# Wide cross attention on one core: the output projection of two batches at once, transposed, and turned back

## The reference, cut to what matters

```python
def _L1_xattn_ref(x, context, ln_gamma, ln_beta, Wq, Wkv, Wo, bo, mask):
    ...
    xn = (x - mu) * jax.lax.rsqrt(var + LN_EPS) * ln_gamma + ln_beta
    q = xn @ Wq                      # 256 -> 1024
    kv = context @ Wkv               # context: 361 rows of 192
    ...
    dots = jnp.einsum('bhnd,bhmd->bhnm', q, k) * scale
    dots = jnp.where(mask, dots, -jnp.inf)
    attn = jax.nn.softmax(dots, axis=-1)
    out = jnp.einsum('bhnm,bhmd->bhnd', attn, v)
    out = out.transpose(0, 2, 1, 3).reshape(x.shape[0], x.shape[1], INNER)
    return out @ Wo + bo             # 1024 -> 256
...
x = x + _L1_xattn_ref(_layernorm(x, axis=-1), ctx_768, ...)
```

## Time and profile before

| | us |
|---|---|
| three runs | 3828.05, 3830.51, 3836.60 (median 3830.51) |
| the profiled execution | 3829.01 |
| its span of engine work | 3827.2 |
| PE busy in the span | 3591.3 (94%) |
| PE's granted clock, mean of the span | 0.965 of full speed |
| DVE, ACT, POOL busy | 1925.8, 1614.7, 1558.3 |

### The profile page before, as it was taken

The page is one execution under the profiler, slowest core; times in us unless marked ns, Lnnn a source line. Parts: engine busy times, 40 slices in busy tenths (PEclk is TensorE's granted clock), DMA queues, the critical chain, the costliest instruction groups (busy, mean ns, idle before and its releaser), DMA issues. The chain is left out here.

```text
span 3827.2 us, 70846 instructions
## 1 busy us (share of the span) xinstructions
PE 3591.3 (94%) x25500; PEld 2497.3 (65%) x25501; DVE 1925.8 (50%) x6165; ACT 1614.7 (42%) x3427; POOL 1558.3 (41%) x2142
## 2 busy tenths in 40 slices
PE   8998899998999977999799999999999989999997
PEld 6776455555777763444466666666666658899986
DVE  4554566664677754565455555555455547211123
ACT  4553455554666404677344444444444431111111
POOL 1000333333577505554255555555555547100025
PEclk9999899999999887999899999999999989999998
DMA  9301111110000063000100000000000001799962
GB/s 287 156 0 26 38 38 37 37 25 12 6 18 17 22 184 79 18 18 14 34 13 7 7 7 11 9 7 7 7 12 7 1 3 55 249 324 329 323 221 78
DMA packets 111410, 262.38 MB, mean 69 GB/s; under 512 B 24003, under 2 KB 70240, under 8 KB 95840
## 3 DMA queue, kind: packets, MB, share of 16 engines
q1 hardware_dynamic: 90208, 224.70, 18.3%
q0 software_dynamic: 16384, 26.29, 2.4%
q10 hardware_dynamic: 4608, 8.39, 0.6%
HBM read 196.61 MB, written 62.65 MB: 68 GB/s over the span
## 5 line engine op out<-in xcount | busy, mean ns | idle before, releaser
L2298 POOL TENSOR_SCALAR wide_probs<-wide_probs,wide_inverse 100x361 f32<-100x361 f32 x512 | 606.1, 1196 | 0.1
L2479 ACT ACTIVATE wide_probs<-wide_probs,wide_least 100x361 f32<-100x361 f32 x512 | 300.9, 589 | 627.4 <-DVE wide_least L2545 627.4
L2545 DVE CUSTOM_DVE_ANT_0 wide_probs<-banks,wide_bias 100x361 f32<-100x361 f32 x512 | 251.7, 529 | 123.5 <-issue 123.5
L2296 POOL TENSOR_TENSOR wide_hold_pool<-eps 100x1 f32<-100x1 f32 x256 | 50.6, 198 | 578.6 <-DVE wide_inverse L2551 577.1
L2354 PE MATMUL banks<-w_wide_v,wide_c 64*120 64x512 f32 (+1 forms) x1152 | 263.5, 589 | 2.5 <-DVE wide_v L2531 1.8
L1978 ACT ACTIVATE rot_h<-banks,w_rot_b 128x800 f32<-128x800 f32 x256 | 223.4, 923 | 87.1 <-PE banks L1852 82.9
L2348 PE MATMUL banks<-wide_c,w_wide_k 64*128 64x361 f32 x1536 | 255.4, 464 | 3.1 <-DVE wide_kT L2528 2.3
L2390 PEld LDWEIGHTS banks<-ident,wide_probs 100*120 100x120 f32 (+1 forms) x1536 | 158.3, 172 | 149.4 <-issue 119.3
L2376 PE MATMUL banks<-wide_kT,wide_qT 64*100 64x361 f32 x1024 | 221.2, 509 | 1.5 <-issue 1.3
L2893 PEld LDWEIGHTS banks<-tiles_xT,tiles_w 128*128 128x128 f32 x1824 | 214.1, 193 | 4.5 <-issue 1.6
L2893 PE MATMUL banks<-tiles_xT,tiles_w 128*128 128x128 f32 x1824 | 214.6, 276 | 1.2 <-DVE tiles_xT L3139 1.2
(11 more groups left out here) (454 smaller groups left out, 7766.0 us busy)
## 6 DMA issues: line engine op xcount, KB each, us to landing
tiles_w<-in_moe_w SPq DMA_DIRECT2D x114, 1024.0 KB, 5.0
slots<-zeros SPq DMA_DIRECT2D x58, 512.0 KB, 5.8
cross_c<-in_ctxT SPq DMA_DIRECT2D x32, 270.8 KB, 4.3
wide_c<-in_ctxT SPq DMA_DIRECT2D x32, 270.8 KB, 4.0
mix_kT<-slots SPq DMA_DIRECT2D x32, 256.0 KB, 4.1
slots<-mix_kT ACTq DMA_DIRECT2D x32, 256.0 KB, 3.8
tiles_rows<-slots SPq DMA_DIRECT2D x57, 128.0 KB, 4.6
slots<-tiles_out SPq DMA_DIRECT2D x57, 128.0 KB, 4.9
```

The lines of the kernel that those rows point to most:

```text
L2298: last = nc.gpsimd.tensor_scalar(t.probs[:, i % RING, j, :], t.probs[:, i % RING, j, :], t.inverse[:, i % RING, j:j + 1], None, ALU.mult)
L2479: last = nc.scalar.activation(t.probs[:, i % RING, j, :], t.probs[:, i % RING, j, :], ACT.Exp, bias=t.least[:, i % RING, j:j + 1], scale=-1.0,
L2545: last = nc.vector.tensor_tensor_reduce(t.probs[:, i % RING, j, :], scores(j), t.bias[:, :], -1.0, LARGEST, ALU.add, ALU.min, t.least[:, i ...
```

## The change

The projection is written the other way around. `headsT` becomes double-buffered over pairs, with both lanes side by side: `[P, 2, WM, LANES, S]`. For each of two 128-column chunks of the output, the eight blocks of the weights are stationary (128 x 128), and the 200 columns of both lanes move past them. The result is the projection transposed (128 output columns by 200 rows, two chunks: 128 x 400). ACT copies it to `projT`; PE turns it back with four transposes into the same bank; DVE adds both lanes.

All of it moves into the first half of the next pair: chunk 0 at the end of item 2, chunk 1 at the end of item 3, ACT's copy in item 3, the transposes and both adds in item 4. `turn_rows` and `keep_rows` go from item 5 to item 6. Nothing is left in item 7 of the second half. For the last pair all of it stands after the last `by_v`. New semaphores: `projT_ready` (PE to ACT), `projT` (ACT to PE), `proj_ready` (PE to DVE), `added`.

```diff
-            def project(of, lane):
-                pe.wait_ge(a[lane * MH + MH - 1].headsT, of.n)
+            def project(of, c):
+                pe.wait_ge(a[ITEMS - 1].headsT, of.n)
                 for m in range(WM):
-                    last = nc.tensor.matmul(side_rows(lane), t.headsT[:, lane, m, :], w.proj[:, m, :], start=(m == 0), stop=(m == WM - 1))
-                last.then_inc(proj_ready[lane], 1)
+                    last = nc.tensor.matmul(side_chunk(c), w.proj[:, m, c * P:(c + 1) * P], t.headsT[:, of.buf, m, :, :].rearrange("p l s -> p (l s)"),
+                                            start=(m == 0), stop=(m == WM - 1))
+                if c == DC - 1:
+                    last.then_inc(s.projT_ready, 1)
+
+            def turn_proj(of):
+                pe.wait_ge(s.projT, of.done)
+                for lane in range(LANES):
+                    for c in range(DC):
+                        at = lane * D + c * P
+                        last = nc.tensor.transpose(side[0:S, at:at + P], t.projT[:, c, lane, :], g.ident[:, :])
+                last.then_inc(s.proj_ready, 1)
...
-                    if here.hf == 0 and i == 3 and before:
-                        pe.wait_ge(added[0], count(pe, here, here.pair))
-                        project(before, 1)
-                    if here.hf == 0 and i == 5 and after and not last_pair(here):
+                    if here.hf == 0 and before:
+                        if i == 2:
+                            project(before, 0)
+                        if i == 3:
+                            project(before, 1)
+                        if i == 4:
+                            turn_proj(before)
+                    if here.hf == 0 and i == 6 and after and not last_pair(here):
                         if before:
-                            pe.wait_ge(added[1], count(pe, here, here.pair))
+                            pe.wait_ge(s.added, before.done)
                         turn_rows(next_pair(pe, here))
-                    if here.hf == 1 and i == 7:
-                        project(here, 0)
...
-            pe.wait_ge(added[0], PAIRS)
-            project(LAST, 1)
+            for c in range(DC):
+                project(LAST, c)
+            turn_proj(LAST)
...
+            def keep_proj(of):
+                act.wait_ge(s.projT_ready, of.done)
+                nc.scalar.copy(t.projT[:, :, :, :].rearrange("p c l s -> p (c l s)"), side[:, 0:DC * LANES * S]).then_inc(s.projT, 1)
...
-            def add(of, lane):
-                lane, b, n = lane_of(dve, of, lane)
-                dve.wait_ge(proj_ready[lane], count(dve, of, of.pair + 1))
-                dve.wait_ge(s.biased, n)
-                nc.vector.scalar_tensor_tensor(g.x[:, b, :], side_rows(lane), t.any[:, :], g.x[:, b, :], ALU.mult, ALU.add).then_inc(added[lane], 1)
+            def add(of):
+                dve.wait_ge(s.proj_ready, of.done)
+                for lane, b, n in [lane_of(dve, of, lane) for lane in range(LANES)]:
+                    dve.wait_ge(s.biased, n)
+                    last = nc.vector.scalar_tensor_tensor(g.x[:, b, :], side_rows(lane), t.any[:, :], g.x[:, b, :], ALU.mult, ALU.add)
+                last.then_inc(s.added, 1)
```

More of the change, by code:

```diff
@@ L2215, in wide_cross_phase @@
     with ExitStack() as ctx:
-        s = semaphores(nc, ctx, "wide", "bias turned_zero any_key any_inverse any y yT_ready yT biased")
+        s = semaphores(nc, ctx, "wide", "bias turned_zero any_key any_inverse any y yT_ready yT biased projT_ready projT proj_ready added")
         made, kept_act, kept_dve = ([ctx.enter_context(nc.semaphore(f"wide_{n}_{k}{i}")) for k, i in UNITS_WIDE] for n in ("made", "kept_act", "kept_dve"))
         a = [semaphores(nc, ctx, f"wide{i}", "scores_ready masked rowsum inverse probs turned_ready probsT_act probsT_dve heads_ready headsT") for i in range(ITEMS)]
-        proj_ready, added = ([ctx.enter_context(nc.semaphore(f"wide_{n}{lane}")) for lane in range(LANES)] for n in ("proj_ready", "added"))
         ctx_loaded = [ctx.enter_context(nc.semaphore(f"wide_ctx_loaded{k}")) for k in range(2)]
@@ L2222, in wide_cross_phase @@
                     v=[TMAX, HALVES, NT, LANES, BANK], qT=[P, HALVES, MH, LANES, S], bias=[S, CTX], least=[S, RING, ITEM], probs=[S, RING, ITEM, CTX],
-                    rowsum=[S, RING, ITEM], inverse=[S, RING, ITEM], probsT=[TMAX, RING, ITEM, NT * S], headsT=[P, LANES, WM, S],
+                    rowsum=[S, RING, ITEM], inverse=[S, RING, ITEM], probsT=[TMAX, RING, ITEM, NT * S], headsT=[P, 2, WM, LANES, S], projT=[P, DC, LANES, S],
                     hold_dve=[S, ITEMS], hold_pool=[S, ITEMS], any_key=[S, 1], any_inverse=[S, 1], any=[S, 1])
@@ L2229, in wide_cross_phase @@
         side_rows = lambda lane: side[0:S, lane * D:(lane + 1) * D]
+        side_chunk = lambda c: side[:, c * LANES * S:(c + 1) * LANES * S]
         rows_of = lambda lane: slice(LANE_ROWS * lane, LANE_ROWS * (lane + 1))
@@ L2235, in half_at @@
             fixed = isinstance(pair, int)
-            return Fields(hf=hf, buf=at % 2, fixed=fixed, pair=pair, n=pair * HALVES + (hf + 1) if fixed else eng.snap(pair * HALVES + (hf + 1)))
+            return Fields(hf=hf, buf=at % 2, fixed=fixed, pair=pair, done=pair + 1 if fixed else eng.snap(pair + 1), n=pair * HALVES + (hf + 1) if fixed else eng.snap(pair * HALVES + (hf + 1)))
         def count(eng, of, value):
@@ L2497, in run @@
                         keep_probs(before, ITEMS - 1)
-                    if here.hf == 0 and i == 5 and after and not last_pair(here):
+                    if here.hf == 0 and i == 3 and before:
+                        keep_proj(before)
+                    if here.hf == 0 and i == 6 and after and not last_pair(here):
                         keep_rows(next_pair(act, here))
@@ L2505, in _ @@
             keep_probs(LAST, ITEMS - 1)
+            keep_proj(LAST)
         @block.vector
@@ L2558, in keep_heads @@
                 dve.wait_ge(a[i].heads_ready, of.n)
-                nc.vector.tensor_copy(t.headsT[:, LANE_OF(i), of.hf * MH + BLOCK_OF(i), :], heads_bank).then_inc(a[i].headsT, 1)
-            def add(of, lane):
-                lane, b, n = lane_of(dve, of, lane)
-                dve.wait_ge(proj_ready[lane], count(dve, of, of.pair + 1))
-                dve.wait_ge(s.biased, n)
-                nc.vector.scalar_tensor_tensor(g.x[:, b, :], side_rows(lane), t.any[:, :], g.x[:, b, :], ALU.mult, ALU.add).then_inc(added[lane], 1)
+                nc.vector.tensor_copy(t.headsT[:, of.buf, of.hf * MH + BLOCK_OF(i), LANE_OF(i), :], heads_bank).then_inc(a[i].headsT, 1)
+            def add(of):
[4 more added lines that the diff above has]
+                last.then_inc(s.added, 1)
             def run(before, here, after):
@@ L2586, in run @@
                         keep_heads(before, ITEMS - 2 + i)
-                    if here.hf == 0 and i == 3 and before:
-                        add(before, 1)
-                    if here.hf == 1 and i == 7:
-                        add(here, 0)
+                    if here.hf == 0 and i == 4 and before:
+                        add(before)
             stats(FIRST)
@@ L2599, in _ @@
             keep_heads(LAST, ITEMS - 1)
-            add(LAST, 1)
+            add(LAST)
 GATHER = 8
```

## The result

| | before | changed |
|---|---|---|
| four runs each, median | 3830.36 us | 3868.84 us (3863.39 to 3877.51) |
| ratio, with 95% interval | | 1.0095 (1.0079 to 1.0111) |
| profiled execution, its span | 3829.01, 3827.2 | 3867.39, 3865.5 |
| PE busy, granted clock of the span | 3591.3, 0.965 | 3593.3, 0.962 |

Forecast were 3817 us and a range of 3809 to 3825. The kernel is slower by far more than the 0.2% that can be told from no change, and slower than any of the rivals.

A forecast was written before the change was run, and what follows sets the result against it. PE was taken to bound the kernel: 3829.0 - 16.5 (projection form) + 2 (loop heads) + 2 (phase end) = 3816.5, predicted as 3817 us, with 3809 to 3825 for 8 in 10.

The forecast's parts named there:

- the rivals: Loop head loses cover (3840 us, 0.06; half-lost 3824 to 3832, 0.10), loads show (3827, 0.03), engine chain (3829 to 3831, 0.05).
- What bounds the kernel: Wide phase's steady part: PE busy 1197.5 of 1199 us, so each us of PE work removed saves a us.
- The form: Projection per pair: -7.24 + 5.62 + 0.52 = -1.10 us (-0.79 to -1.35); 15 pairs give -16.5 us.
- The loads are hidden: Projection records: time goes by moving columns, wider stationary loads lie under the matmul ahead; 2.81 us per 16 records.
- The rival in which 22 ns of each load show: Projection records: wider loads add 22 ns each, a pair loses 0.70 of its 1.10 us; 3827 us, chance 0.03.
- The covers: First halves: item chain, ACT's copy, DVE's adds and later turn_rows stay behind PE's work, costing nothing.
- The loop heads: Branch after item 7 of second halves, only short by_v queued last: 0.3 us in each of seven rounds, +2 us (0 to +9).
- The row I leaned on: First block's loop: a first group starting without idle behind one short projection, taken as showing a short queue at a branch.
- The loop head loses its cover: Branch after item 7 of second halves: up to 3.6 us laid bare in 7 rounds, +25, 3840 us; chance 0.06, half-lost 0.10.
- The end of the phase: After the last item, projection no longer fills PE's wait for POOL: +1.2 us plus slower clock, +2 us (1.2 to 4.5).

The follow-up runs named there:

- shifted changed kernel: The changed kernel with 32 more PE instructions (rounds of long-fulfilled waits) ahead of the wide phase's loop, same work; ratio 1.0050 to the kernel before.
- moved branch: The changed kernel with PE's loop branch moved to after item 3 of a first half, behind the second projection chunk; ratio 0.9990 to the kernel before.
- shifted kernel before: The kernel before with 224 more PE instructions (rounds of long-fulfilled waits) ahead of the wide phase's loop, same work; ratio 1.0143 to the kernel before.

## Why the prediction was wrong, point by point

**What bounds the kernel: right.** PE stayed the limit, and a us less of PE work was a us less of time wherever no branch lay between.

**The form: right, size a little off.** -0.87 us a pair instead of -1.10, inside the bounds (-0.79 to -1.35). A projection took 2.90 instead of 2.81, the distance that I had named as the dearer end; the turn took 0.57 instead of 0.52, between 100 columns' 0.49 and the scaled 0.63. Together -13.1 instead of -16.5.

**The loads are hidden: right.** 2.90 / 16 = 181 ns a record with 128 stationary, 0.91 ns a column, against 226 ns for 256 columns with 100 stationary. The rival in which 22 ns of each load show would have given 198 ns. The Trainium skill's rule that a load overlaps only with another row group (TensorE: Matmul & The Clock Gate, Part 3, "The mechanism") isn't borne out by these records, 181 ns each beside loads of 190. The same section also lets a load into the background weight buffer go ahead of matmuls in flight, and that these records would fit.

**The covers: right.** PE has no wait for `projT`, DVE's adds or POOL in the first halves. ACT's copy took 492 ns. The item chain behind the shortened stretch held.

**The loop heads: the step that failed.** The term was +2 us, 0.3 for each of seven rounds, on the ground that a short queue at a branch shows no idle; measured +47.9, 8.0 for each of six. The row I leaned on the earlier trace rows was misread. Its time, 67.64 us, lies in straight code: PE enters the first block's loop at 106.6 and branches back first at 168.1. At the true branches of that loop PE doesn't stand either, but there was nothing to fetch. Over its two branches, from 168 to 291 us, the DMA view of the kernel before reads

```profile
DMA packets 0, 0.00 MB, mean 0 GB/s; under 512 B 0, under 2 KB 0, under 8 KB 0
```

and over one round of the wide loop, 2112.2 to 2268.8 us,

```profile
q8 instruction: 11, 0.18, 0.4%
```

A round of the first block's loop is 1002 recorded PE instructions, and the longest other loop without an instruction packet on q8 has 1326 (541.9 to 843.0 us). The wide loop has 2475. So short loops ran without a new fetch and the long one is fetched anew each round; where the limit lies between 1326 and 2475 no run shows, nor what a round of one pair instead of two would do.

The right row was in hand: the earlier trace rows had the two packets, and the packet's moment against the scores' start gives 2.9 us. The idle there was 0.37 behind a whole projection; leave only `by_v` and the end of the transposes, and from the issue of the branch 3.95 - 1.34 = 2.6 us must show. That alone is 6 x 2.3 = +14 over before, and uses up the gain of the form. The shifted changed kernel is in just this state, with 3.0 us a head.

**The rival named the place but not the size.** "The loop head loses its cover" was capped at what the cover had hidden, 3.6 us. It could not hold the other two parts, which have no row in the kernel before: the second page, which came because removed code moved the target, and the clock. By the distances a head costs 8.28 us now and 2.98 with the target moved back, so the place and what follows of it are 5.3 of the 8.3. At the head shown, which cost 86.44 - 77.21 = 9.2, it is 2.7 in the first stand, 3.7 from the scores to the query unit (4.53 us instead of 0.79: the second stand, and matmuls at half speed) and 2.7 in the query unit (5.49 instead of 2.81). One number of that rival was off too: it leaves no gain from (16.5 - 2) / 7 = 2.1 us a round on, not from 1.8.

**The end of the phase: right in kind, low in size.** Forecast +2 (1.2 to 4.5), measured +4.5, the far end: the 32 records took 8.12 us, where 5.81 is full clock, so 2.3 us are half clock, where I gave it 0.8. With the 1.2 of the forecast and 0.2 for the dearer records that is 3.7; the other 0.8 isn't broken down.

**What is shown and what is argued.** Shown: the stands are tied to the fetch (packets), to the branch (gone without it), to the queued work (2.4 to 3.0, 1.2 to 1.5 and 0.2 to 0.7 us with 1.3, 2.9 and 3.6 us left when the branch is issued), and the second one to the program's place (comes and goes with shifted code alone). Argued: that the target lies just ahead of a page's end. A second packet moves 0.2 to 0.3 us after PE goes on in the kernel before and in the shifted one too, without a second stand; only with the target at the changed kernel's place does PE stop for it, 2.2 to 2.9 us, after one score matmul. That the half clock follows from the stands is also argued, from their standing together: two stands with one matmul between were followed by it at all 18 heads in three kernels, one stand at one head of six. Open: what besides the clock spreads the runs of the shifted changed kernel, and the 3.3 us behind the phase.

## What to carry to other kernels

Before removing or moving work at the end of a loop's body on the limiting engine, read the fetch from the trace (packet to first instruction, here 2.9 us; issue of the branch to first instruction, here 3.7 to 4.4) and set it against what stays queued there; a long group of matmuls ahead of a branch is not in the way, it is the cover. When straight code or a loop on that engine changes length, look at the loop heads again, since the target's place alone made 31 us here by the traces and some 18 by the medians. Look also whether the loop is fetched at all: count its instructions and the packets in one round. If it is, and the program is short enough, write it out: a rewrite that lost 1% with the loop gained 0.3% without, and 0.5% once its end was given the old order.

## What the runs showed of the hardware that I had not expected

- After a taken branch back of the wide loop, PE's first instruction came 2.7 to 3.3 us after its page's packet moved (up to 3.4 at the moved branch). The Trainium skill (Runtime: NRT & Kernel Launch, "Instruction fetch mechanics") says that a branch out of the loaded pages must fetch first; by that rule, the trace agrees. The same section puts what is loaded at 2048 instructions for PE and, in another sentence, at two pages of 256. The first fits this trace and the second doesn't: rounds of 1002 and 1326 instructions went without a fetch, rounds of 2475 did not. Without branches on PE, 74 packets went by with 0.2 us of idle in all.
- 32 instructions more or less ahead of a loop, doing nothing, moved a head's cost between 3.0 and 8.3 us in the profiled executions.
- PE issued the branch with 15 to 17 matmul records still to run, in all seven kernels with a loop on PE, whether they were 256 or 100 columns long. So long matmuls ahead of a branch cover more.
- One stand of 2.5 to 2.8 us left the granted clock at 1.00 at five heads of six, and 2.88 us at the sixth was followed by the low clock. 0.42 and 2.25 us with one matmul between them, or 2.74 and 1.58, were followed by 5 us and more at 0.50, the level of 1.2 GHz (3 us and more at all 18 heads with two stands):

```profile
2418.50:2422.50 4.00, 3.92 (x24) 3.42 (x25) 1.28 (x7) 1.39 (x5) 0.45 (x2) 1.00 0.02 4
```

```profile
2459.00:2464.50 5.50, 5.50 (x17) 5.39 (x17) 1.16 (x6) 1.27 (x4) 2.53 (x3) 0.50 0.01 3
```

The first is behind the one stand of the shifted changed kernel, the second behind the two of the shifted kernel before.
